# Choosing the experts on the logits, and computing their gates behind the first gathers

## Chip, cores and metric

The kernel runs on one core of a Trainium2 chip. The metric is the device time of one execution in microseconds (us), the median of three runs.

## What is computed

One transformer layer on 16 x 224 = 3584 tokens of 512 values: cross attention on 750 context rows per batch entry, and then a mixture of 8 experts, two per token, each expert taking at most 1120 tokens.

```python
x = x + xattn(layernorm(x), ctx, mask, W_q, W_k, W_v, W_o, b_o)
xf = layernorm(x).reshape(t, D)
probs = softmax(xf @ Wr)
topk_probs, topk_experts = top_k(probs, 2)
for e in range(8):
    mask = topk_experts == e
    gate = sum(where(mask, topk_probs, 0.0))
    vals, idx = top_k(where(any(mask), gate, -inf), cap)      # cap = 1120
    h = relu(xf[idx] @ W1[e]) @ W2[e]                         # 512 -> 2048 -> 512
    y = y.at[idx].add(where(isfinite(vals), vals, 0)[:, None] * h)
x = x + y
```

## The kernel before

**Attention.** `build` first runs `preamble`, which finds from the mask which keys can matter and puts a flag in `T["flag"]`. All engines load that flag and branch: `attention_short` when it is 1, else `attention_general`. The short version is the one that runs on this input. It handles two batch entries in an iteration: the first iteration is written out, six run in a loop, the last is written out. It leaves the router's logits in SBUF, `T["logits"]`, laid out as 112 partitions x 8 experts x 32 token tiles, so 256 columns; the normalized rows go to DRAM as `xn2_rows`. In the instruction streams the branch taken on 1 stands first, the other behind it, and `router` follows.

**Weights.** All products of the experts run as three products on numbers split in a high and a low part. An expert's weights come in 8 pairs of chunks, 1 MB each, through a double buffer `stage`: SyncE loads a pair (`load_pair`), ScalarE writes the high part (`split_pair_hi`, four pieces of 128 x 512), VectorE or GpSimd the low part (`split_pair_lo`, L942). SyncE loads a pair only once the pair two before has its low part. For expert 0, pairs 0 and 1 are loaded in `router` and their high parts made there; GpSimd makes the low parts of pairs 0 to 3, ahead of its first gather, VectorE that of pair 4, and pairs 5 to 7 are split inside block 0 (`refresh`).

**Router** (L945 to L1055). GpSimd makes constant tables with iotas. VectorE waits for all five, copies them, and computes the softmax over the experts (ScalarE does the exponential), then in two rounds the largest probability, its expert (`sel`), and masks it out (`rest`). `has` marks the two chosen experts of each token, `gate` their probabilities. `vals` is a table of four values per token and expert: token number, gate high, gate low, 1. TensorE sums the counts over partitions. If an expert has more than 1120 tokens, `threshold` selects among them by gate; it doesn't run on this input. Each of `router`, `threshold` and `experts` is a block whose end all five engines wait for.

**Slots** (in `experts`). A scan and a product on TensorE give each chosen token its position in its expert (L1349 to L1359, L1477, L1478). VectorE splits the position in a tile number and a row (`slot_tile`, `slot_row`). For an expert, `slot_tiles` compares tile numbers (`eq_t`), `slot_moves` multiplies these with `vals` (`moves`, 1152 columns), and `slot_onehot` makes, eight times, one-hot tables of the rows of four token tiles; TensorE multiplies them (`slot_product`, 4 products of 36 columns each into `psI`), and `slot_ids` turns the result into gather ids, scatter ids and gates. For expert 0 this runs before the first gather; for a later expert it is spread over the 16 steps of the middle block of the expert before (`next_slots`).

**Experts.** An expert has 3 blocks of 3 token tiles, 24 blocks in all. GpSimd gathers the rows of a block from `xn2_rows` by indirect DMA (`xg`), TensorE transposes them (`turn`, `psX`), ScalarE and VectorE write high and low part (`xgT`, `split_x`). A block has 16 steps: TensorE computes `psH` (`hidden`), ScalarE the high part of its relu, VectorE the low part (`hT_lo`, L1390), and TensorE adds the step before to `psY` (`output`). If an expert's counts allow it, a block runs only two of its three tiles. VectorE multiplies `psY` with the gates (`y_out`), GpSimd scatters with addition. VectorE also clears three PSUM banks before block 0 (L1355).

```python
        with nc.If(flag_value(nc, T) == 1):
            attention_short(nc, T, A)
        with nc.Else():
            attention_general(nc, T, A)
```

## Time and profile before

| | |
|---|---|
| median of 3 timed runs | 2272.09 us (2270.47 to 2272.11) |
| profiled execution | 2268.47 us, span 2266.7 us |
| TensorE busy | 2097.9 us (93%) |
| VectorE, ScalarE, GpSimd busy | 994.7 (44%), 677.9 (30%), 511.5 (23%) |
| mean granted TensorE clock | 0.981 of full speed |

The span is what the profiler saw between the first and the last instruction. "Busy" leaves out waits. Idle time of an engine matters only where the chain of work that ends last runs through it. The granted clock is 1.0 at 2.4 GHz and 0.5 at 1.2 GHz.

### The profile page before, as it was taken

What the parts mean: (1) busy time and instruction counts of PE and PEld (TensorE: products, weight loads), DVE (VectorE), ACT (ScalarE), POOL (GpSimd) and SP (SyncE); (2) the same over time, 40 slices, a digit from 0 to 9 for tenths busy, and PEclk for the clock granted to TensorE, in tenths of its full rate; (3) what the DMA queues carried; (4) which work ended last, traced back from release to release, by engine and by line L of the source; (5) the groups of instructions that cost most, each with busy time, mean ns of one, the idle gap of its engine ahead of it and who ended that gap; (6) DMA issues with size and microseconds to landing.
All of it is one profiled execution on the core that took longest, in us unless ns stands there. A gap on an engine that the chain in (4) does not pass through costs nothing.

```text
span 2266.7 us, 30701 instructions
## 1 busy us (share of the span) xinstructions
PE 2097.9 (93%) x12006; PEld 1857.3 (82%) x12006; DVE 994.7 (44%) x2207; ACT 677.9 (30%) x1672; POOL 511.5 (23%) x551
## 2 busy tenths in 40 slices
PE   4898898898896399999999999999999999999997
PEld 3877877877884399899989889998888899988997
DVE  5665666666665633422422342242224345224221
ACT  3533633633542222311321131132113124113110
POOL 1542543543543411110101111010110111110100
PEclk9999999999997599999999999999999999999999
DMA  4122022022012332420421242042124325113211
GB/s 142 48 80 67 13 79 69 11 79 72 7 49 71 120 84 46 133 54 14 119 73 28 46 133 54 14 121 71 28 42 132 60 45 160 27 33 122 41 14 15
DMA packets 95533, 148.40 MB, mean 65 GB/s; under 512 B 7920, under 2 KB 49312, under 8 KB 95376
## 3 DMA queue, kind: packets, MB, share of 16 engines
q1 hardware_dynamic: 79632, 109.36, 15.1%
q0 software_dynamic: 15744, 36.71, 9.2%
q8 instruction: 127, 2.08, 0.4%
q14 instruction: 30, 0.25, 0.0%
HBM read 110.66 MB, written 35.39 MB: 64 GB/s over the span
## 4 chain that ended last, share of the span: by engine, by line
PE 65%; DVE 1%; issue 1%; DMA 0%; POOL 0%; POOLq 0%; ACT 0%; DVEq 0%
PE psH L1410 31%; PE psY L1410 31%; PE psX L1424 1%; PE psI L1455 1%; DMA xg<-xn_rows,gid 0%; DVE onehot L1307 0%; POOL out_dram L1236 0%; POOL xg L1227 0%; DVE moves L1299 0%; POOLq L1157 0%; DVE xg L1349 0%; DVE xg L1369 0%; DVE xg L1352 0%; DVE ys L1364 0%; DVE w_lo L942 0%
## 5 line engine op out<-in xcount | busy, mean ns | idle before, releaser
L1390 DVE SCALAR_TENSOR_TENSOR hT_lo<-psH,hT_hi 128x384 fp32r<-128x384 f32 (+1 forms) x384 | 209.9, 546 | 944.6 <-ACT hT_hi L1266 939.2
L1266 ACT ACTIVATE hT_hi<-psH 128x384 fp32r<-128x384 f32 (+1 forms) x384 | 185.2, 482 | 1124.5 <-PE psH L1410 1119.2
L1410 PE MATMUL psH<-xgT_hi,w_hi 128*128 128x384 f32 (+2 forms) x1536 | 484.8, 316 | 9.5 <-issue 8.8
L1410 PE MATMUL psH<-xgT_lo,w_hi 128*128 128x384 f32 (+2 forms) x1536 | 482.9, 314 | 4.9 <-issue 4.9
L1410 PE MATMUL psH<-xgT_hi,w_lo 128*128 128x384 f32 (+2 forms) x1536 | 484.0, 315 | 0.0
L1410 PE MATMUL psY<-w_hi,hT_hi 128*128 128x512 f32 (+1 forms) x1002 | 402.7, 402 | 0.0
L1410 PE MATMUL psY<-w_hi,hT_lo 128*128 128x512 f32 (+1 forms) x1002 | 394.2, 393 | 0.0
L1410 PE MATMUL psY<-w_lo,hT_hi 128*128 128x512 f32 (+1 forms) x1002 | 394.1, 393 | 0.0
L1410 PEld LDWEIGHTS psH<-xgT_hi,w_hi 128*128 128x128 f32 x1536 | 290.5, 189 | 33.8 <-issue 17.4
L1410 PEld LDWEIGHTS psH<-xgT_lo,w_hi 128*128 128x128 f32 x1536 | 290.6, 189 | 21.0 <-issue 5.7
L1410 PEld LDWEIGHTS psH<-xgT_hi,w_lo 128*128 128x128 f32 x1536 | 290.3, 189 | 0.0
L1227 POOL DMA_INDIRECT xg<-xn_rows,gid x72 | 71.6, 994 | 871.5 <-PE psX L1424 506.5
L1410 PEld LDWEIGHTS psY<-w_hi,hT_lo 128*128 128x128 f32 (+1 forms) x1002 | 187.0, 187 | 43.0
L1236 POOL DMA_INDIRECT out_dram<-ys,sid x72 | 114.5, 1590 | 441.9 <-DVE ys L1336 427.3
L1410 PEld LDWEIGHTS psY<-w_lo,hT_hi 128*128 128x128 f32 (+1 forms) x1002 | 187.9, 188 | 28.7
L1410 PEld LDWEIGHTS psY<-w_hi,hT_hi 128*128 128x128 f32 (+1 forms) x1002 | 188.0, 188 | 27.3
L375 ACT ACTIVATE probs<-probs,nmax 112x250 f32<-112x250 f32 x256 | 126.7, 497 | 111.3 <-DVE nmax L477 111.3
L942 DVE TENSOR_TENSOR w_lo<-stage,w_hi 128x512 fp32r<-128x512 f32 x240 | 154.8, 687 | 1.0 <-ACT w_hi L937 1.0
L937 ACT ACTIVATE w_hi<-stage 128x512 fp32r<-128x512 f32 x256 | 146.1, 624 | 22.2 <-DMA stage<-in_L_ffn_W_dram 22.2
L332 POOL TENSOR_TENSOR probs<-probs,rsum 112x500 f32<-112x500 f32 x128 | 130.6, 1020 | 10.0
L330 POOL TENSOR_TENSOR rsum<-ssum,minus_one 112x2 f32<-112x2 f32 x128 | 89.6, 700 | 131.5 <-ACT probs L375 131.5
L549 PE MATMUL psO<-pT_hi,v_hi 125*128 125x224 f32 x256 | 81.5, 318 | 38.3 <-DVE pT_lo L490 38.3
(187 smaller groups left out, 2965.6 us busy)
## 6 DMA issues: line engine op xcount, KB each, us to landing
stage<-in_L_ffn_W_dram SPq DMA_DIRECT2D x128, 512.0 KB
x_sb<-in_x_dram SPq DMA_DIRECT2D x8, 896.0 KB, 8.1
x_res<-in_x_dram SPq DMA_DIRECT2D x8, 896.0 KB, 5.7
out_dram<-x_res SPq DMA_DIRECT2D x8, 896.0 KB, 4.8
xn_rows<-xn SPq DMA_DIRECT2D x8, 896.0 KB, 4.8
c_sb<-in_ctx_dram SPq DMA_DIRECT2D x16, 375.0 KB
out_dram<-zrow SPq DMA_DIRECT2D x9, 256.0 KB, 4.4
xg<-xn_rows,gid POOLq DMA_INDIRECT x72
```

Source lines behind the costliest of these rows:

```text
L330: nc.gpsimd.tensor_tensor(rsum[:, u % 4, :], ssum[:, u % 4, :], T["minus_one"][0:R, :], ALU.pow).then_inc(recip, 1)
L332: nc.gpsimd.tensor_tensor(P[:, u % 4], P[:, u % 4], rsum[:, u % 4, :].unsqueeze(2).to_broadcast([R, 2, NKEY]), ALU.mult).then_inc(normed, 1)
L375: e = nc.scalar.activation(P[:, i % 4, it, :], P[:, i % 4, it, :], ACT.Exp, bias=nmax[:, i % 4, it:it + 1], scale=-1.0, accum_out=ssum[:, ...
L549: mm = nc.tensor.matmul(out, stationary(a, c), moving(b, c), start=first and c == 0 and j == 0, stop=last and c == n - 1 and j == 2, skip_ ...
L937: nc.scalar.activation(piece(T, 0, pair, j), staged(T, pair, j), ACT.Copy).then_inc(T["w_hi_done"], 1)
L942: engine.tensor_tensor(piece(T, 1, pair, j), staged(T, pair, j), f32(piece(T, 0, pair, j)), ALU.subtract).then_inc(T["w_lo_done"], 1)
L1227: nc.gpsimd.indirect_dma_start(out=xg[0:m, t, :], out_offset=None, in_=A["xn2"], in_offset=bass.IndirectOffsetOnAxis(ap=gid[e % 2][0:m, c: ...
L1236: nc.gpsimd.indirect_dma_start(out=A["out"], out_offset=bass.IndirectOffsetOnAxis(ap=sid[e % 2][0:m, c:c + 1].bitcast(U32), axis=0), in_=y ...
L1266: nc.scalar.activation(hT[0][:, f % 2, 0:m], psH[f % 2][:, 0:m], ACT.Relu).then_inc(h_hi, 1)
L1390: nc.vector.scalar_tensor_tensor(out=hT[1][:, f % 2, 0:m], in0=psH[f % 2][:, 0:m], scalar=0.0, in1=f32(hT[0][:, f % 2, 0:m]), op0=ALU.max, ...
L1410: mm = nc.tensor.matmul(out, stationary(a, c), moving(b, c), start=first and c == chunks[0] and j == 0, stop=last and c == chunks[-1] and ...
L1424: mm = nc.tensor.transpose(psX[c % 2][:, at:at + m], xg[0:m, t, c * 128:(c + 1) * 128], T["ident"][0:m, 0:m])
```

## The change

Seven parts:

1. `build`: the branches are swapped, `attention_general` stands first in the streams and `attention_short` directly ahead of `router`.
2. `router` chooses on the logits (`select`) instead of on the softmax; its VectorE waits first only for one iota, and the other table copies move behind the counts.
3. The ranks (scan, subtraction, two products, `ranks_before`, `positions`) move from `experts` into `router`.
4. The softmax and gates (`gates`, `exponentials`) and the filling of `vals` move into `experts`, behind the ids of expert 0.
5. Position to tile and row: tile numbers stay multiplied by 128, which needs no shift and one cast less (five steps for seven).
6. Expert 0 has an early table of ids only (`early_slots`, `early_ids`, 10 columns); its full table with gates is made in block 0 (`next_slots(0, f)`, `slot_product(0, f - 4)`).
7. GpSimd splits no weights: VectorE makes the low parts of pairs 0 and 1 before block 0; pairs 2 to 7 are split in block 0.

```diff
 build
-            with nc.If(flag_value(nc, T) == 1):
-                attention_short(nc, T, A)
-            with nc.Else():
-                attention_general(nc, T, A)
+            with nc.If(flag_value(nc, T) == 0):
+                attention_general(nc, T, A)
+            with nc.Else():
+                attention_short(nc, T, A)
...
 router, GpSimd
-            for pair in range(EARLY_LO):
-                for j in range(PIECES):
-                    split_pair_lo(nc.gpsimd, T, 0, pair, j)
...
 router, VectorE
+            dve.wait_ge(iotas, 1)
+            nc.vector.tensor_copy(W["rank"][:], rank_i[:])
+            select(dve, nc, T, W, then)
+            then(nc.vector.tensor_tensor(T["has"][:], W["sel"][:, 0], W["sel"][:, 1], ALU.add))
+            nc.vector.tensor_reduce(cnt[:], T["has"][:], AX.X, ALU.add).then_inc(counts, 1)
+            then(nc.vector.tensor_copy(T["keep"][:], T["has"][:]))
+            dve.wait_ge(consts, 5)
+            ranks_before(dve, nc, T, then, marks)
+            dve.wait_ge(counted, 1)
...
 router, ScalarE
-            act.wait_ge(shifted, 1)
-            nc.scalar.activation(z[:], z[:], ACT.Exp).then_inc(exped, 1)
             for pair in range(EARLY):
                 for j in range(PIECES):
                     split_pair_hi(act, nc, T, 0, pair, j)
...
 router, TensorE
             nc.tensor.matmul(ps[0:R, 0:E], T["ones_m"][:], cnt[:], start=True, stop=True).then_inc(counted, 1)
+            positions(pe, nc, T, marks, placed)
+            pe.wait_ge(placed, 1)
...
 experts
-                return (0, BEFORE + f // 2, 2 * (f % 2)) if f < 2 * (WPAIRS - BEFORE) else None
+                return (0, EARLY + f // 2, 2 * (f % 2)) if f < 2 * (WPAIRS - EARLY) else None
...
 experts, GpSimd
-            for pair in range(EARLY_LO, POOL_PAIRS):
-                for j in range(PIECES):
-                    split_pair_lo(nc.gpsimd, T, 0, pair, j)
             gather(0)
...
 experts, ScalarE
-            for pair in range(EARLY, BEFORE):
-                for j in range(PIECES):
-                    split_pair_hi(act, nc, T, 0, pair, j)
+            exponentials(act, nc, T, shifted, exped)
...
 experts, VectorE
+            def early_slots():
+
+                slot_tiles(0)
+                dve.wait_ge(eq_done, 1)
+                nc.vector.tensor_tensor(early_ids[:], eq_t[:], T["ids"][:].unsqueeze(2).to_broadcast([R, NT, EVEN]),
+                                        ALU.mult).then_inc(early_done, 1)
+                for q in range(GROUPS):
+                    slot_onehot(0, 0, q)
+                dve.wait_ge(slot_mm, GROUPS)
+                nc.vector.tensor_copy(gid[0][:], psI[:, 0:CAPT]).then_inc(ids_ready, 1)
...
+            then(nc.vector.scalar_tensor_tensor(out=T["slot_tile"][:], in0=pos, scalar=1.0, in1=T["keep"][:], op0=ALU.add, op1=ALU.mult))
+            then(nc.vector.tensor_scalar(T["pos_i"], T["slot_tile"][:], -1.0, None, ALU.add))
+            then(nc.vector.tensor_scalar(T["row_i"], T["pos_i"], 127, None, ALU.bitwise_and))
+            then(nc.vector.tensor_copy(T["slot_row"][:], T["row_i"]))
+            then(nc.vector.scalar_tensor_tensor(out=flat(T["slot_tile"][:]), in0=flat(T["slot_tile"][:]), scalar=-1.0,
+                                                in1=flat(T["slot_row"][:]), op0=ALU.add, op1=ALU.subtract))
+            early_slots()
             for bank in (*psH, psY[BLK - 1]):
                 s = nc.vector.memset(bank[:], 0.0)
             s.then_inc(cleared, 1)
...
+            gates(dve, nc, T, then_gate, shifted, exped)
...
-            dve.wait_ge(T["w_lo_done"], PIECES * POOL_PAIRS)
-            for pair in range(POOL_PAIRS, BEFORE):
+            for pair in range(EARLY):
                 for j in range(PIECES):
                     split_pair_lo(nc.vector, T, 0, pair, j)
...
+                    if n == 0:
+                        next_slots(0, f)
                     if k == 1 and e + 1 < E:
                         next_slots(e + 1, f)
...
 experts, TensorE
+                    if n == 0 and 4 <= f < 4 + GROUPS:
+                        slot_product(0, f - 4)
```

The new function that chooses:

```python
def select(dve, nc, T, W, then):
    rank, red, eq, sel = W["rank"], W["red"], W["eq"], W["sel"]
    src = T["logits"]
    for k in range(2):
        then(nc.vector.tensor_reduce(red[:, k, :], over_experts(src[:]), AX.X, ALU.max))
        then(nc.vector.tensor_tensor(eq[:], src[:], each_expert(red[:, k, :]), ALU.is_equal))
        then(nc.vector.tensor_tensor(eq[:], eq[:], rank[:], ALU.mult))
        then(nc.vector.tensor_reduce(red[:, 2, :], over_experts(eq[:]), AX.X, ALU.max))
        then(nc.vector.tensor_tensor(sel[:, k], rank[:], each_expert(red[:, 2, :]), ALU.is_equal))
```

After the first round it masks the chosen logit with -BIG, into `rest`, as the code before did with -2.

**How the order moves.** The end of attention on VectorE before (`logits` is the last result, the rows behind the branches are the general version):

```order
L506 COPY x2T<-psT 128x4x112 x4
L510 COPY lgT<-psJ 8x448
L512 COPY logits<-psJ 112x4x8
L199 UNCONDITIONAL_BRANCH
L1558 UNCONDITIONAL_BRANCH
L753 UNCONDITIONAL_BRANCH
L756 UNCONDITIONAL_BRANCH
L756 ISA
L766 TENSOR_SCALAR g_mask_bias<-g_m 112x750
```

and now:

```order
L506 COPY x2T<-psT 128x4x112 x4
L510 COPY lgT<-psJ 8x448
L512 COPY logits<-psJ 112x4x8
L199 UNCONDITIONAL_BRANCH
L1619 UNCONDITIONAL_BRANCH
L1034 UNCONDITIONAL_BRANCH
L1045 CAST rank<-rank_i 112x256
L947 TENSOR_REDUCE red<-logits 112x32
L948 TENSOR_TENSOR eq<-logits,red 112x256
```

The router's first step now follows attention's last one; the general version stands ahead of attention.

The start of the expert block on VectorE before, from the scan to the low parts of a weight pair:

```order
L1349 SCALAR_TENSOR_TENSOR xg<-xg 112x256
L1352 TENSOR_TENSOR xg<-xg 112x256
L1355 MEMSET psH 128x512 x2
L1355 MEMSET psY 128x512
L1359 CAST ys<-psI 112x256
L1361 TENSOR_SCALAR ys<-ys 112x256
L1363 CAST slot_tile<-ys 112x256
L1364 TENSOR_SCALAR ys<-ys 112x256
L1366 CAST xg<-ys 112x256
L1369 SCALAR_TENSOR_TENSOR xg<-xg 112x256
L1372 TENSOR_SCALAR slot_row<-xg 112x256
L1290 TENSOR_TENSOR eq_t<-iota_t,slot_tile 112x288
```

and now, up to the first step of the gates:

```order
L1402 SCALAR_TENSOR_TENSOR slot_tile<-psI,xg 112x256
L1403 TENSOR_SCALAR xg<-slot_tile 112x256
L1404 TENSOR_SCALAR xg<-xg 112x256
L1405 CAST slot_row<-xg 112x256
L1406 SCALAR_TENSOR_TENSOR slot_tile<-slot_tile,slot_row 112x256
L1323 TENSOR_TENSOR eq_t<-iota_t,slot_tile 112x320
L1348 TENSOR_TENSOR early_ids<-eq_t,ids 112x320
L1340 TENSOR_TENSOR onehot<-iota,slot_row 112x512 x8
L1353 CAST gid<-psI 128x9
L1410 MEMSET psH 128x512 x2
L1410 MEMSET psY 128x512
L962 TENSOR_REDUCE ys<-logits 112x32
```

The scan left this place; one copy stands between the one-hot tables and the ids; the PSUM clears and the gates follow behind it.

Block 0 on VectorE now (each `hT_lo` begins a step of the block):

```order
L1436 SCALAR_TENSOR_TENSOR hT_lo<-psH,hT_hi 128x352
L939 TENSOR_TENSOR w_lo<-stage,w_hi 128x2x256 x2
L1436 SCALAR_TENSOR_TENSOR hT_lo<-psH,hT_hi 128x352
L939 TENSOR_TENSOR w_lo<-stage,w_hi 128x512 x2
L1436 SCALAR_TENSOR_TENSOR hT_lo<-psH,hT_hi 128x352
L939 TENSOR_TENSOR w_lo<-stage,w_hi 128x2x256 x2
L1332 TENSOR_TENSOR moves<-eq_t,vals 112x1152
L1436 SCALAR_TENSOR_TENSOR hT_lo<-psH,hT_hi 128x352
L939 TENSOR_TENSOR w_lo<-stage,w_hi 128x512 x2
L1340 TENSOR_TENSOR onehot<-iota,slot_row 112x512
```

In the order before, these steps held `hT_lo` and, for six of them, `w_lo` alone; `moves` and the one-hot tables stood ahead of the block.

## Rows read from the trace of the kernel before

**Rows 1.** Windows view: us; busy (x) PE, PEld, DVE, ACT, POOL; clock; DMA; GB/s.

```profile
722.00:785.00 63.00, 13.70 (x52) 11.48 (x53) 41.44 (x74) 13.21 (x25) 29.84 (x31) 0.51 0.40 129
```

**Rows 2.** Timeline (start, duration, engine, line, operation, idle before): attention ends, router starts.

```profile
721.49 0.21 DVE L512 COPY logits<-psJ 112x32 f32<-112x32 f32 x1 [0.54 <-PE psJ L606]
...
722.15 0.42 SPq L929 DMA_DIRECT2D stage<-in_L_ffn_W_dram  x1
...
722.46 0.38 POOL L973 IOTA rank_i<- 112x256 int32 x1 [11.34 <-POOLq L199]
...
726.29 0.29 DVE L1002 CAST rank<-rank_i 112x256 f32<-112x256 int32 x1 [4.59 <-issue]
```

**Rows 3.** DMA queues, 722 to 724 us: packets, MB, share of 16 engines.

```profile
q14 instruction: 3, 0.02, 3.6%
```

**Rows 4.** DMA queues, 220 to 640 us: all that moved packets.

```profile
q1 hardware_dynamic: 12989, 22.22, 17.6%
```

**Rows 5.** Timeline of the choice of experts: GpSimd, then VectorE.

```profile
730.25 5.49 POOL L942 TENSOR_TENSOR w_lo<-stage,w_hi 128x512 fp32r<-128x512 f32 x4 [6.00 <-ACT w_hi L937]
...
734.66 1.37 DVE L1023 SCALAR_TENSOR_TENSOR rest<-sel,router_probs 112x256 f32<-112x256 f32 x1
...
736.06 0.58 DVE L1016 TENSOR_REDUCE red<-rest 112x32 f32<-112x256 f32 x1
...
738.67 0.42 DVE L1026 TENSOR_TENSOR xg<-sel 112x256 f32<-112x256 f32 x1
```

**Rows 6.** Timeline of VectorE, the ranks in the expert block.

```profile
743.38 1.38 DVE L1349 TENSOR_TENSOR_SCAN xg<-xg 112x256 f32<-112x256 f32 x1 [1.46 <-PEq L947]
744.79 1.30 DVE L1352 TENSOR_TENSOR xg<-xg 112x256 f32<-112x256 f32 x1
746.20 1.03 DVE L1355 MEMSET psH<- 128x512 f32 x2
...
748.23 0.42 DVE L1359 CAST ys<-psI 112x256 int32<-112x256 f32 x1 [0.47 <-PE psI L1478]
```

**Rows 7.** Timeline of ScalarE, the last weight split of the router.

```profile
732.15 2.19 ACT L937 ACTIVATE w_hi<-stage 128x512 fp32r<-128x512 f32 x4 [0.42 <-DMA stage<-in_L_ffn_W_dram]
```

**Rows 8.** Timeline of the slots of expert 0: VectorE, TensorE, VectorE, GpSimd.

```profile
754.23 0.29 DVE L1372 TENSOR_SCALAR slot_row<-xg 112x256 f32<-112x256 f32 x1
...
762.45 5.54 PE L1455 MATMUL psI<-moves,onehot 112*128 112x36 f32 x24 [0.64 <-DVE onehot L1307]
...
768.03 0.20 DVE L1320 COPY slot<-psI 128x36 f32<-128x36 f32 x1 [1.14 <-PE psI L1455]
...
769.73 1.40 POOL L1227 DMA_INDIRECT xg<-xn_rows,gid  x1 [7.88 <-DVE slot L1327]
```

**Rows 9.** Timeline from the gathers to the first product.

```profile
769.33 2.50 DVE L942 TENSOR_TENSOR w_lo<-stage,w_hi 128x512 fp32r<-128x512 f32 x4
...
779.80 1.44 PE L1424 MATMUL psX<-ident,xg 128*128 128x128 f32 x6 [11.81 <-DMA xg<-xn_rows,gid]
...
781.18 1.11 DVE L1283 TENSOR_TENSOR xgT_lo<-psX,xgT_hi 128x352 fp32r<-128x352 f32 x2 [9.35 <-ACT xgT_hi L1255]
...
784.36 0.63 PE L1410 MATMUL psH<-xgT_hi,w_hi 128*128 128x352 f32 x1 [1.16 <-issue]
```

**Rows 10.** Timeline of VectorE in block 1.

```profile
842.13 1.35 DVE L1299 TENSOR_TENSOR moves<-eq_t,vals 112x1152 fp32r<-112x1152 f32 x1
844.47 0.56 DVE L1390 SCALAR_TENSOR_TENSOR hT_lo<-psH,hT_hi 128x384 fp32r<-128x384 f32 x1 [1.00 <-ACT hT_hi L1266]
...
847.29 0.56 DVE L1390 SCALAR_TENSOR_TENSOR hT_lo<-psH,hT_hi 128x384 fp32r<-128x384 f32 x1 [1.66 <-ACT hT_hi L1266]
...
850.55 0.56 DVE L1390 SCALAR_TENSOR_TENSOR hT_lo<-psH,hT_hi 128x384 fp32r<-128x384 f32 x1 [2.10 <-ACT hT_hi L1266]
```

**Rows 11.** Waits after 786 us: who waited for whom, total us, times, longest.

```profile
ACT w_hi L937 <- DMA stage<-in_L_ffn_W_dram: 1.0, 1, 1.0
```

**Rows 12.** Costliest groups: count, busy us, mean ns, idle before.

```profile
L1227 POOL DMA_INDIRECT xg<-xn_rows,gid x72 | 71.6, 994 | 871.5 <-PE psX L1424 506.5
```

More of the change, by code:

```diff
@@ L998, in then @@
                 dve.wait_ge(step, done[0])
-            logits = T["logits"]
+            dve.wait_ge(iotas, 1)
[7 more added lines that the diff above has]
+            dve.wait_ge(counted, 1)
+            then(nc.vector.tensor_reduce(over[:, 0:1], ps[0:1, 0:E], AX.X, ALU.max))
+            then(nc.vector.tensor_scalar(over[:, 1:2], over[:, 0:1], float(CAP) + 0.5, None, ALU.is_gt))
+            then(nc.vector.tensor_copy(T["flag"][:], over[:, 1:2]))
+            for k in range(NBLK):
+                m = nc.vector.tensor_scalar(more[:, :, k], ps[0:1, 0:E], TILES[k][-1] * 128 + 0.5, None, ALU.is_gt)
+            then(m)
+            nc.vector.tensor_copy(T["more"][:], more[:].rearrange("p e k -> p (e k)"))
             dve.wait_ge(iotas, 5)
-            nc.vector.tensor_copy(rank[:], rank_i[:])
             nc.vector.tensor_copy(T["iota"][:], iota_i[:])
@@ L1033, in _ @@
-            dve.wait_ge(counted, 1)
-            for k in range(NBLK):
-                nc.vector.tensor_scalar(more[:, :, k], ps[0:1, 0:E], TILES[k][-1] * 128 + 0.5, None, ALU.is_gt)
-            then(nc.vector.tensor_reduce(over[:, 0:1], ps[0:1, 0:E], AX.X, ALU.max))
-            then(nc.vector.tensor_scalar(over[:, 1:2], over[:, 0:1], float(CAP) + 0.5, None, ALU.is_gt))
-            nc.vector.tensor_copy(T["more"][:], more[:].rearrange("p e k -> p (e k)"))
-            then(nc.vector.tensor_copy(T["flag"][:], over[:, 1:2]))
@@ L1041, in _ @@
[L1041 removed]
+            then(nc.vector.tensor_copy(T["ids"][:], id_i[:]))
         @block.scalar
         def _(act):
[L1045 to L1046 removed]
             for pair in range(EARLY):
@@ L1474, in more @@
                                       max_val=1, skip_runtime_bounds_check_because="it is a comparison's result")
-            pe.wait_ge(marks, 1)
-            nc.tensor.matmul(psI[0:R, 0:E * NT], T["after"][:], flat(T["keep"][:]), start=True, stop=False)
-            nc.tensor.matmul(psI[0:R, 0:E * NT], T["ones_m"][:], flat(before[:]), start=False, stop=True).then_inc(placed, 1)
             for q in range(GROUPS):
-                slot_product(0, q)
+                early_product(q)
             for c in range(DCH):
```

195 lines of the change are left out of this document (103 added, 92 removed).

## Prediction

> **What bounds the kernel now.** I read the busy time by stretches first, then the chain of waits, then each engine's timeline between the end of attention and the first expert block. Attention (to 722 us) and the expert blocks (from 785 us) are TensorE at work. Between them lie 63 us in which TensorE is busy 13.7 us and its granted clock is 0.51, the lower level (1.2 GHz), while VectorE is busy 41 us [rows 1]. In this stretch the chain of waits runs through VectorE's router and slot steps, then the first gathers, then TensorE. Everything after hangs on the moment at which the first `psH` product starts, 784.36 us, and follows at TensorE's pace. So I work out that start anew, then what block 0 gets to do in addition.
>
> **1. Entry to the router.** Attention's last VectorE operation starts at 721.49; SyncE passes the barrier and issues at 722.15, GpSimd makes `rank_i` at 722.46 (0.38 us), but VectorE starts only at 726.29, 4.59 us of "issue" [rows 2]. At that moment instruction packets are fetched [rows 3]: VectorE leaves `attention_short` by a jump over the general version, some 340 rows of its order. The change swaps the two branches, so VectorE falls into the router. Its first operation then needs only `rank_i`: 722.9, 3.4 us earlier. If the stall had another cause, the 3.4 us stay in this step.
>
> The same jump is now taken at the start of the kernel, before attention's first loads are used. Bounds: 0 (target already fetched) and 3.4 us (as at the end). I take 0: six passes of attention's loop, five jumps back on every engine, show no instruction packet at all from 220 to 640 us [rows 4], so a jump to code that is held costs no fetch, and the weight loads that the stalled fetch had beside it are not there yet.
>
> **2. Choosing on the logits.** GpSimd no longer splits weights. Its 5.49 us group from 730.25 on covered part of the choice: the two-input step at 734.66 took 1.37 us, one of the same 256 columns at 738.67, with GpSimd idle, 0.42 [rows 5]. I price all at the second kind. One round of choosing is 736.06 to 738.67 = 2.61 us. Forward from 722.9 (a two-input step counts 0.46, its 0.42 and 0.04 to the next): cast 0.2, two rounds 5.22, masking 0.46, `has` 0.46, count and `keep` 0.76, which gives 730.0. The softmax and the tables of gates are no longer ahead of it. The scan ran 1.38 us beside GpSimd [rows 6]; its bounds are 0.42 and 1.38, I take 0.42 because every other two-input step of this size that I could read both ways fell to it. Scan and subtraction: 0.92, the two position products 2.13 (746.10 to 748.23) [rows 6]: positions at 733.1, at most 734.0.
>
> **3. What is late next.** The router's block ends when all engines reach its end. ScalarE still splits weight pairs 0 and 1 there, and their loads start no earlier than now: its last group starts at 732.15 and takes 2.19 [rows 7], until 734.3. That was hidden (VectorE went on to 741.9); now it is last by 1.2 us. So 1.2 us of step 1 and 2's gain is lost, and an error there under 1.2 us costs nothing. VectorE stood idle 1.46 us between the two blocks (the scan's idle time, [rows 6]); same barrier, same load of the flag, same jump over `threshold`: 735.8.
>
> **4. Slots of expert 0.** Two steps of two inputs at 0.46, three of one input at 0.33 (0.29 and the 0.04 to the next) [rows 8], and two on 320 columns at 0.54: 3.0, so 738.8. The 4-value table `moves` is off this path. Eight one-hot tables follow at the rate of uncontended 512-column subtractions, 2.50 for four [rows 9]: 5.0, and 1.1 from the last to the result (idle time of 1.14, [rows 8]). Bounds: TensorE took 5.54 for 24 products of 36 columns, 0.92 per table [rows 8]; 10 columns cannot take more, so at most 0.7 + 8 times 0.92 = 8.1 in all, at least 6.1. I take 6.1, as the products shrink to 10 columns: 744.9. The ids then need one copy, 0.2 in place of eight small steps, and 0.3 to GpSimd: first gather at 745.4 against 769.73 [rows 8], **24.3 us earlier**.
>
> **5. Behind the gathers.** Gather to turn took 10.1 us (to 779.80), turn to the first product 4.6 [rows 8, 9]. VectorE meanwhile runs three PSUM clears (two took 1.03 [rows 6], so 1.6), the gates (eleven steps and ScalarE's exponential, 0.42 each as in rows 5: 5.1), and now both early pairs' subtractions, 8 at 0.63 = 5.0. From 745.1 it is free at 756.8. It is wanted at 745.4 + 11.45 = 756.85 (781.18 less 769.73) [rows 9]. The two paths are level: cover used up, nothing lost. Faster gathers would gain nothing, a VectorE 1 us later costs 1 us. First product: 760.1, still 24.3 earlier.
>
> **6. Block 0 pays.** The full slot product of expert 0 moves into block 0. In block 1, where such products already stand, the step between `hT_lo` starts is 2.82 us without one (844.47 to 847.29) and 3.26 with one (847.29 to 850.55) [rows 10]: 8 times 0.44 = 3.5. VectorE has now in one step `hT_lo` 0.56, two subtractions 1.3 and `moves` 1.35 [rows 9, 10] = 3.2, 0.4 over 2.82. In the next step its first one-hot table ends 0.5 (ScalarE's half) + 0.56 + 1.3 + 0.7 after the product, and 0.4 late: 3.4 where TensorE asks at 2.8. That is 0.6, once. Together +4.1.
>
> Pairs 2 to 7 are now loaded and split in block 0, two pieces per step. Need: 1 MB in two steps, 5.64 us or more. Supply: 2 MB issued from 722.15 were in at 732.15, 5.0 per pair [rows 2, 7]; in the later experts at the same pace ScalarE waited for a load once, 1.0 us [rows 11]. Cost 0, with about 1 us to spare for each.
>
> **Sum.** -24.3 + 4.1 = **-20.2 us**. The profiled execution took 2268.47 (span 2266.7 and 1.8 around it), 3.6 below the median of the three timed runs, 2272.09. So 2248.3 for such an execution, and **2251.9** against the median.
>
> **Rivals.**
>
> *The jump at the start stalls too.* +3.4 on the path, since VectorE's first statistics open attention. For: the stall at 722 to 726 with its fetch. Against: rows 4. Gives 2255.3. The Trainium skill (Runtime: NRT & Kernel Launch, Instruction fetch mechanics) says that fetching is sequential, that a taken branch out of the two-block window stalls, and that the window is 512 instructions on most engines, 2048 on TensorE. By that rule the target at the start lies inside the window and the cost is 0. No row here shows the window's size.
>
> *Weights late in block 0.* The second gather group now shares the queues with pairs 3 and 4, and a pair's load may start only when the pair two before is subtracted, about 6.5 us ahead of its use. If such a load takes 8.5 us (1.7 MB at 5.0 per MB), each of five pairs is 2 us late: +10. Gives 2261.9.
>
> *Descriptors held up.* GpSimd's gather instruction took 1.40 us beside VectorE's subtractions, on average 0.99 [rows 8, 12]. If each of the three waits 0.5 us behind the copies and casts of the gate steps, the turn is 1.4 later: 2253.3. The Trainium skill (SBUF — State Buffer, Who interferes with whom) says that copies and casts in a two-port mode lock GpSimd out of descriptor writing, so it speaks against computing the gates behind the gathers.
>
> *Contention was not GpSimd's.* If VectorE's steps stay at their long durations, 0.95 us more on each of six such steps of the new path, 5.7 us come back, less the 1.2 of step 3: 2256.4. Against: rows 5.
>
> *Slower: attention's loop refetches.* The swap moves the loop's code by some 340 rows on VectorE, more on TensorE. If it then no longer fits what is held, each of the five jumps back stalls. At 4.6 us, the gap of rows 2, that is 23, and 3.4 for the start: -20.2 + 26.4 = +6.2, 2278.3. It decides from 4.0 us per jump. Against: the loop is no longer than before, and no fetch shows in it now.
>
> **How the numbers follow.** Forecast 0.65; start jump 0.13; weights late 0.10; descriptors 0.04; contention stays 0.04; refetch 0.03; 0.01 for none of these. A measurement here tells 0.2% (4.5 us) from no change. All cases but refetch and the rest are faster by more: 0.94 faster, 0.03 same, 0.03 slower. Range: below, a ScalarE that ends 1.2 earlier, no 0.6 in block 0, and the spread of the medians of about 2 us give 2247; above it reaches to the late weights, 2262.
>
> **What would show it.** VectorE's first router step near 722.9 plus any loss at the start; the router's block ending with ScalarE's pair 1; one-hot tables 0.63 apart; first gather 24 us earlier counted from attention's end; `moves` and eight slot products inside block 0 and steps of 3.3 us. ScalarE waiting for `stage` in block 0, a first attention step later than before, or instruction packets from 220 to 640 us would show me wrong.

## The result, and the profile after

The changed kernel took **2240.13 us** (median of 4 runs, 2237.11 to 2241.82) against 2272.09 before; the ratio is 0.9866 (95% interval 0.9848 to 0.9884). The forecast was 2251.9 with a range of 2247 to 2262: the direction was right, the gain of 32 us is 12 us more than forecast and outside the range. The profiled execution took 2237.11 us (span 2235.4, granted clock 0.987), against 2268.47 (span 2266.7).

I cut both traces at the same eight moments: the first VectorE operation of attention, attention's last `logits`, the router's first operation, the first gather's issue, the first `psH` product of block 0, and the first `ys` of blocks 0, 1 and 23 (each is one row's start, each figure a difference of two starts; the `ys` of a block are made while TensorE is already at the next one).

| stretch, us | before | after | difference | forecast |
|---|---|---|---|---|
| to attention's first VectorE operation | 15.31 | 18.57 | +3.3 | 0 |
| attention, to its last `logits` | 706.2 | 702.2 | -4.0 | 0 |
| to the router's first operation | 4.80 | 0.94 | -3.9 | -3.4 |
| router and slots, to the first gather | 43.4 | 23.2 | -20.2 | -20.9 |
| gather to first product | 14.6 | 14.5 | -0.2 | 0 |
| first product to the first `ys` of block 0 | 52.5 | 57.4 | +4.9 | +4.1 |
| first `ys` of block 0 to that of block 1 | 51.3 | 51.4 | 0.0 | 0 |
| from there to the first `ys` of block 23 | 1366.8 | 1355.6 | **-11.2** | 0 |

The sum is -31.3. The first `ys` of block 0 came 20.15 us earlier, as forecast (-20.2), but partly by luck: the start lost 3.3 us that I had put at nothing, and attention, in which nothing was changed, was 4.0 us shorter. The miss is the last line.

The start and the entry to the router, timeline of VectorE after (start, duration, engine, line, operation, idle before):

```profile
18.57 0.69 DVE L427 BATCH_NORM_STATS2 st<-x_sb 112x6 f32<-112x512 f32 x1 [14.13 <-issue]
...
720.72 0.21 DVE L512 COPY logits<-psJ 112x32 f32<-112x32 f32 x1 [0.54 <-PE psJ L606]
721.65 0.41 DVE L1045 CAST rank<-rank_i 112x256 f32<-112x256 int32 x1 [0.73 <-POOL rank_i L1020]
```

The stall of [rows 2] is gone (0.73 us of idle time in place of 4.59, and its end is GpSimd's `rank_i`), and the start shows one instead: ScalarE and SyncE begin attention at 15.17 us in both kernels, VectorE at 18.57 in place of 15.31, and between 0 and 20 us instruction packets are fetched (two on queue q14, one on q8) where the kernel before has none.

The router and slots on VectorE, then the weights on ScalarE, then the first gather on GpSimd, the turn on TensorE and VectorE's work behind the gather:

```profile
728.77 0.69 DVE L980 TENSOR_TENSOR_SCAN xg<-xg 112x256 f32<-112x256 f32 x1
729.50 0.43 DVE L981 TENSOR_TENSOR xg<-xg 112x256 f32<-112x256 f32 x1
...
733.52 0.42 DVE L1402 SCALAR_TENSOR_TENSOR slot_tile<-psI,xg 112x256 f32<-112x256 f32 x1 [2.28 <-PEq L994]
...
738.15 0.69 DVE L1340 TENSOR_TENSOR onehot<-iota,slot_row 112x512 fp32r<-112x512 f32 x1 [0.51 <-PE psI L1504]
739.00 0.69 DVE L1340 TENSOR_TENSOR onehot<-iota,slot_row 112x512 fp32r<-112x512 f32 x1 [0.16 <-PE psI L1504]
```
```profile
727.12 2.19 ACT L934 ACTIVATE w_hi<-stage 128x512 fp32r<-128x512 f32 x4 [31.37 <-DMA stage<-in_L_ffn_W_dram]
730.10 2.19 ACT L934 ACTIVATE w_hi<-stage 128x512 fp32r<-128x512 f32 x4 [0.79 <-DMA stage<-in_L_ffn_W_dram]
```
```profile
744.88 1.24 POOL L1265 DMA_INDIRECT xg<-xn_rows,gid  x1 [21.66 <-DVE gid L1353]
746.42 0.96 POOL L1265 DMA_INDIRECT xg<-xn_rows,gid  x1 [0.30 <-issue]
```
```profile
751.21 1.44 PE L1472 MATMUL psX<-ident,xg 128*128 128x128 f32 x6 [6.85 <-DMA xg<-xn_rows,gid]
756.74 1.43 PE L1472 MATMUL psX<-ident,xg 128*128 128x128 f32 x6 [4.09 <-DVE xgT_lo L1316]
759.34 0.63 PE L1458 MATMUL psH<-xgT_hi,w_hi 128*128 128x352 f32 x1 [1.16 <-issue]
```
```profile
751.35 4.91 DVE L939 TENSOR_TENSOR w_lo<-stage,w_hi 128x512 fp32r<-128x512 f32 x8
756.17 0.95 DVE L1316 TENSOR_TENSOR xgT_lo<-psX,xgT_hi 128x352 fp32r<-128x352 f32 x2
```

Operations of 256 columns run at their short times (0.43 where [rows 6] had longer ones); the scan takes 0.69. The one-hot tables come 0.85 and 0.95 apart, each held up by TensorE's product. The gather now lands after 6.3 us (10.1 before), and then TensorE waits 4.09 us for VectorE, which is still at the weights.

In the later blocks the difference is idle time of TensorE without a releaser. The groups of instructions between 870 and 2225 us (busy us, mean ns, idle before), of the kernel before, then of the changed one:

```profile
L1410 PE MATMUL psH<-xgT_hi,w_hi 128*128 128x384 f32 (+2 forms) x1400 | 443.7, 317 | 7.8 <-issue 7.1 <-DVE w_lo L942 0.6
L1410 PE MATMUL psH<-xgT_lo,w_hi 128*128 128x384 f32 (+2 forms) x1401 | 442.4, 316 | 4.9 <-issue 4.9
```
```profile
L1458 PE MATMUL psH<-xgT_hi,w_hi 128*128 128x384 f32 (+2 forms) x1400 | 444.2, 317 | 3.4 <-issue 3.3
L1458 PE MATMUL psH<-xgT_lo,w_hi 128*128 128x384 f32 (+2 forms) x1400 | 442.5, 316 | 0.0
```

So 12.0 us of "issue" before and 3.3 after, 8.7 of the 11.2 us; the mean product is the same. In TensorE's timeline of the kernel before they are single gaps (the four longest are shown), two of them in the middle of a group of three products on the same tiles:

```profile
959.56 0.39 PE L1410 MATMUL psH<-xgT_hi,w_hi 128*128 128x256 f32 x1 [2.40 <-issue]
...
1679.88 0.44 PE L1410 MATMUL psH<-xgT_lo,w_hi 128*128 128x384 f32 x1 [1.97 <-issue]
...
1754.78 0.38 PE L1410 MATMUL psH<-xgT_hi,w_hi 128*128 128x256 f32 x1 [1.68 <-issue]
...
1806.06 0.39 PE L1410 MATMUL psH<-xgT_lo,w_hi 128*128 128x256 f32 x1 [2.04 <-issue]
```

The branches that answer to the first and the third in the changed kernel:

```profile
936.41 0.39 PE L1458 MATMUL psH<-xgT_hi,w_hi 128*128 128x256 f32 x1 [0.24 <-issue]
...
1726.78 0.39 PE L1458 MATMUL psH<-xgT_hi,w_hi 128*128 128x256 f32 x1 [1.34 <-issue]
```

Each of them lies within 5 us of a block's end, where TensorE's program branches on `more(n)` or jumps over the variant of the steps that it did not run. TensorE's instructions come as packets on DMA queue q8, and one starts 2.4 to 2.8 us before each of the four gaps ends (at 957.2, 1677.5, 1752.3 and 1803.3). DMA queues around the last gap, 1797 to 1809 us, and around the same place of the changed kernel, 1769 to 1781 us (packets, MB, share):

```profile
q8 instruction: 4, 0.07, 2.2%
```
```profile
q8 instruction: 2, 0.03, 1.0%
```

While blocks 2 to 23 ran, the kernel before fetched 104 packets for TensorE, the changed kernel 98. The two kernels' instructions of one block are the same; what differs is how many stand ahead of it: the early products, and a slot product in both variants of block 0.

**Theory A**: the gaps are instruction fetches, and which branches have one depends on where they stand in the packets that the instructions come in (16 KB each: 127 packets, 2.08 MB on queue q8 of the kernel before). **Rival B**: the earlier gathers and loads, or another part of the change, took contention away. **Rival C**: such gaps vary from one execution to the next.

### The profile page after: what moved, and what is told of

Its sections match the earlier page's. It is cut to its first block, busy times and chain, and to the rows that moved or that the text cites. A ratio compares the mean times of both kernels' runs of the same rounds, so it can differ in the third digit from the quotient of the medians.

```text
span 2235.4 us, 30763 instructions
## 1 busy us (share of the span) xinstructions
PE 2096.5 (94%) x12038; PEld 1860.0 (83%) x12038; DVE 996.3 (45%) x2223; ACT 678.0 (30%) x1672; POOL 488.8 (22%) x535
## 4 chain that ended last, share of the span: by engine, by line
PE 65%; DVE 1%; issue 0%; POOL 0%; POOLq 0%; ACT 0%; DVEq 0%
PE psH L1458 31%; PE psY L1458 31%; PE psX L1472 1%; PE psI L1514 1%; DVE w_lo L939 0%; PE psI L1504 0%; POOL out_dram L1274 0%; POOLq L1196 0%; DVE moves L1332 0%; DVE onehot L1340 0%; DVE psH L1410 0%; DVE hT_lo L1436 0%; DVE ys L1380 0%; DVE ys L965 0%; DVE eq_t L1323 0%
## 5 line engine op out<-in xcount | busy, mean ns | idle before, releaser
L939 DVE TENSOR_TENSOR w_lo<-stage,w_hi 128x512 fp32r<-128x512 f32 x256 | 164.9, 687 | 0.4 <-ACT w_hi L934 0.4
L934 ACT ACTIVATE w_hi<-stage 128x512 fp32r<-128x512 f32 x256 | 146.4, 625 | 32.5 <-DMA stage<-in_L_ffn_W_dram 32.5
```

Of the source, the lines that this page charges most:

```text
L934: nc.scalar.activation(piece(T, 0, pair, j), staged(T, pair, j), ACT.Copy).then_inc(T["w_hi_done"], 1)
L939: engine.tensor_tensor(piece(T, 1, pair, j), staged(T, pair, j), f32(piece(T, 0, pair, j)), ALU.subtract).then_inc(T["w_lo_done"], 1)
```

## Experiments

All times are medians; "against before" is the difference to the kernel before as timed beside it on the same chip (its median was 2268.9 to 2270.6 us there). "Blocks 2 to 23" is the last line of the table above, in the profiled execution.

| run | us | against before | blocks 2 to 23 |
|---|---|---|---|
| before_shift134 | 2268.3 | -2.2 | 1369.7 |
| after_shift122 | 2246.3 | -24.2 | 1361.9 |
| after_order | 2236.5 | -34.0 | 1355.2 |
| before_nopool | 2258.1 | -12.4 | 1373.1 |
| before_shift144 | 2258.3 | -12.3 | 1360.5 |
| after_shift112 | 2249.4 | -21.3 | 1367.6 |
| after_gates_late | 2239.9 | -30.8 | 1356.1 |
| before_nopool_shift144 | 2246.6 | -23.8 | 1359.6 |
| after_again | 2239.1 | -31.3 | 1355.8 |
| after_gates_sp | 2237.9 | -32.5 | 1354.6 |
| after_gates_sp_order | 2238.9 | -31.5 | 1356.4 |
| after_shift32 | 2247.2 | -21.7 | 1360.8 |
| after_shift64 | 2250.0 | -18.9 | 1364.8 |
| after_shift192 | 2252.9 | -16.0 | 1369.8 |
| after_shift224 | 2248.1 | -20.9 | 1365.5 |

### A padding that moved hardly anything

```diff
@@ threshold, TensorE: behind the last product
+            for _ in range(67):
+                nc.tensor.matmul(ps[0:R, E * NT:E * NT + E], T["ones_m"][:], cnt[:], start=True, stop=True)
```

Expected of it in the kernel before:

> The kernel before, with 67 products (134 instructions) added to TensorE's block of the general routing step, which is jumped over and never runs; every instruction of the expert blocks now stands where it stands in the changed kernel from block 1 on. Theory A (the 11 us that the changed kernel gained in blocks 2 to 23 come from where its TensorE branches fall in the instruction fetch): 9 to 11 us faster than the kernel before, all of it in blocks 2 to 23; the gaps of 2.40, 1.97, 1.68 and 2.04 us without a wait at 959.6, 1679.9, 1754.8 and 1806.1 us go, and one of some 1.3 us comes at block 15. Rival B (earlier timing of transfers, less contention): no difference, the gaps stay where they are. Rival C (they vary from one execution to the next): gaps of the same sum at other places.

And of the changed kernel with 61 such products:

> The changed kernel, with 61 products (122 instructions) added in the same block that never runs, so that its expert blocks stand 256 instructions (one packet of 16 KB) behind those of the kernel before. Theory A, if the pattern repeats with the packet: 9 to 11 us slower than the changed kernel, with gaps of 2 us again near the blocks 3, 13, 15 and 16. Rivals B and C: the same time as the changed kernel within 2 us.

Measured: ratio 0.9986 (0.9974 to 0.9998) for the first, with gaps left at blocks 3, 14 and 16 (1.94, 2.10 and 2.59 us); the second 6 us slower than the changed kernel (3.15 us at 1520.05, 1.94 at 2229.19), not at the blocks named. By the letter, theory A was refuted by the first. But the instruction packets told that the edit had not done what I meant: they came where they came before it in a block, to within 2 us. The cause stands in the traces: a product of plain float32 runs as two passes (one product of `positions`, and the one of the counts, each have two rows), each a weight load and a product. So 67 products take 268 places and 61 take 244, and with a packet of 256 instructions that is a shift of +12 and of -12: the two packets inside block 2 started 0.1 and 1.1 us earlier in the one kernel and 1.9 and 1.1 us later in the other. (The Trainium skill, Runtime: NRT & Kernel Launch, Instruction fetch mechanics, gives blocks of 16 KiB with 256 instructions; the trace agrees.) Theory A was hardly tested, though the second run has gaps of 1.94 and 3.15 us that no profile of the changed kernel has.

### The same padding at the right size

36 products (144 places) in the kernel before, 28 (112 places) in the changed one; nothing else.

> The first padding was nearly a whole packet: the rows show a product of plain float32 as two passes, so 67 products took 268 places in the instruction stream, 12 more than the 256 of a 16 KB packet, and the packets of TensorE's instructions came 0.1 to 1.1 us earlier in a block, where those of the changed kernel come 11 us later. This is the kernel before with 36 such products (144 places) in the general routing step that never runs, so that the packets fall in each expert block as in the changed kernel (45.6 us behind the start of block 2's third part in place of 35.1). Theory A (the 11 us in blocks 2 to 23 come from where the branches stand in the packets): 9 to 11 us faster than the kernel before, all in blocks 2 to 23. Rival B (transfers and their timing, the other parts of the change): no faster, gaps of about 2 us stay at blocks 3, 13, 15 and 16.

> The changed kernel with 28 such products (112 places) in the step that never runs, so that the packets fall as in the kernel before. Theory A: 9 to 11 us slower than the changed kernel, in blocks 2 to 23, with gaps of about 2 us near the starts of blocks 3, 13, 15 and 16. Rival B: the changed kernel's time within 2 us.

The packets went where they were meant to: behind the first `ys` of block 1, one starts 35.1 us later in the kernel before, 45.1 with the padding, 45.6 in the changed kernel, 35.2 in the changed kernel with its padding. That of the padded kernel before, DMA queues from 929.5 to 931.5 us (packets, MB, share):

```profile
q8 instruction: 1, 0.02, 4.0%
```

The kernel before became 12.3 us faster (ratio 0.9955, 0.9937 to 0.9974) by instructions that never run. "All in blocks 2 to 23" was not so: these took 6.3 us less in the profiled execution, whose whole span was 9.3 us shorter (attention 2.4, the router and slots 0.9 of it), and the rest of the 12.3 is not located. The packets fetched in blocks 2 to 23 fell from 104 to 98, the gaps at blocks 13 and 16 went, those at blocks 3 and 15 shrank from 2.40 and 1.68 us to 1.22 and 1.00. At block 3:

```profile
954.51 0.39 PE L1412 MATMUL psH<-xgT_hi,w_hi 128*128 128x256 f32 x1 [1.22 <-issue]
```

The changed kernel with the padding became 9 to 10 us slower, with 12.0 us more in blocks 2 to 23, most of it at blocks 3, 13, 14 and 16. In block 3:

```profile
937.71 0.28 PE L1460 MATMUL psH<-xgT_hi,w_lo 128*128 128x256 f32 x1 [3.09 <-issue]
```

Here 104 packets came in blocks 2 to 23. Theory A holds from both sides, and rival B falls for this part: the transfers, the other engines' programs and the order of the work are the same in each pair. Rival C falls as the whole cause, since the medians moved beyond their intervals both times. But it holds in part: single executions of the kernel before took 2262.3 to 2275.1 us, and its version without splits on GpSimd (below), with the same TensorE program and the same 104 packets, took 1373.1 us in blocks 2 to 23 where the kernel before took 1366.8. And the two profiles of the changed kernel show 0.24 and 0.85 us of "issue" at block 3. How long a stall lasts varies from one execution to the next.

A gap can cost more than itself. In the run before_shift134 the granted clock fell to 0.5 for 3.4 us and for 6.8 us at the gaps of blocks 14 and 16, and block 16 took 57.2 us, in place of 51.3 without a gap. Not every gap does this, and its length alone does not decide it: the clock stayed at 1.0 through the gaps of 1.97 to 2.40 us of the kernel before and through those of 3.15 and 3.17 us in after_shift122 and after_shift64, and fell for 3.4 us at one of 1.77 us in after_shift112.

### The circle of positions

The changed kernel with 8, 16, 48 and 56 such products (32, 64, 192 and 224 places).

> The changed kernel with 8 products of plain float32 (32 places) in the general routing step that never runs. Theory A: the time goes by where the branches stand in the packets, most positions cost less than that of the kernel before: 2240 to 2246 us, and the packets come 3 us earlier in each block. Rival (only the position of the kernel before is bad): 2237 to 2242 us.

> The same with 16 products (64 places). Theory A: between the changed kernel and its version with 112 places (2249 us), 2240 to 2250 us, packets 6.5 us earlier in each block. Rival: 2237 to 2242 us.

> The same with 48 products (192 places), 64 places short of a whole packet. Theory A: 2237 to 2250 us, packets 6.5 us later in each block than in the changed kernel. Rival: 2237 to 2242 us.

> The same with 56 products (224 places), 32 places short of a whole packet. Theory A: by the run with 244 places (2246 us, 6 us above the changed kernel, though its packets came only 1 us later) 2242 to 2248 us. Rival: 2237 to 2242 us, and the 2246 us were another chip's.

With the runs above, by places behind the changed kernel, modulo 256: 2239 and 2240 us at 0, 2247 at 32, 2250 at 64, 2249 at 112, 2253 at 192, 2248 at 224, 2246 at 244. Those at 32 and 192 were 1 and 3 us over what theory A had been given, the other two at its upper end; the rival's 2237 to 2242 is out for all, and so is another chip as the reason, since the kernel before took 2268.9 us beside these four and 2270.5 beside the run at 244. The changed kernel stands at the best of the seven positions tried, the kernel before (near 110) among the bad ones. The blocks that lose most change: 0 and 3 at 32, 9 and 18 at 64, 3 and 16 at 112, 4 and 15 at 192, 10 and 21 at 224. At 32 the longest gap of all runs, 3.96 us, stands in block 0, which took 3.9 us more there to its first `ys` than in the changed kernel (61.3 for 57.4); the table's last column does not have it. The packets fetched in blocks 2 to 23 were 98 in all eight kernels at or near 0, 103 or 104 in the four at 110 to 122, and 101, 105, 102, 100 and 97 at 32, 64, 192, 224 and 244. So they go with the time, but roughly. At 192, TensorE's groups between 818 and 2240 us:

```profile
L1460 PE MATMUL psH<-xgT_hi,w_lo 128*128 128x384 f32 (+2 forms) x1465 | 463.4, 316 | 4.1 <-issue 4.1
L1460 PE MATMUL psH<-xgT_hi,w_hi 128*128 128x384 f32 (+2 forms) x1464 | 463.3, 316 | 10.1 <-issue 9.9
```

Why a given position stalls at a given branch stays open.

### No weight splits on GpSimd, alone

```diff
-EARLY_LO = 1
-POOL_PAIRS = 4
-BEFORE = 5
+EARLY_LO = 0
+POOL_PAIRS = 0
+BEFORE = 2
...
-            dve.wait_ge(T["w_lo_done"], PIECES * POOL_PAIRS)
```

> The kernel before with one part of the change alone: no weight splits on GpSimd (VectorE makes the low parts of pairs 0 and 1 ahead of block 0, the others are made in block 0 as in the changed kernel). As I priced the contention (router and slot operations of 0.4 us that took 1.25 to 1.4): the router's and the slots' VectorE work shrinks by some 13 us and the first gather is issued near 757 in place of 769.7; block 0 gives 4 us back, so 8 to 9 us faster in all. Rival (the contention was not GpSimd's splits but the loads' writes): operations stay at 1.25 to 1.4 us, no gain, and 4 us slower.

Measured 12.4 us faster (ratio 0.9938, 0.9921 to 0.9954). From the router's first operation to the gather it took 31.8 us in place of 43.4. The second group of GpSimd's splits in the kernel before, and three position steps on VectorE beside it:

```profile
748.75 5.17 POOL L942 TENSOR_TENSOR w_lo<-stage,w_hi 128x512 fp32r<-128x512 f32 x4 [0.31 <-ACT w_hi L937]
...
749.02 1.25 DVE L1363 CAST slot_tile<-ys 112x256 f32<-112x256 int32 x1
750.18 1.35 DVE L1364 TENSOR_SCALAR ys<-ys 112x256 int32<-112x256 int32 x1
751.57 1.23 DVE L1366 CAST xg<-ys 112x256 f32<-112x256 int32 x1
```

The scan (1.38 us in [rows 6]) and the same three steps now, at short times:

```profile
738.79 0.69 DVE L1349 TENSOR_TENSOR_SCAN xg<-xg 112x256 f32<-112x256 f32 x1 [1.46 <-PEq L947]
...
742.87 0.29 DVE L1363 CAST slot_tile<-ys 112x256 f32<-112x256 int32 x1
743.08 0.28 DVE L1364 TENSOR_SCALAR ys<-ys 112x256 int32<-112x256 int32 x1
743.40 0.29 DVE L1366 CAST xg<-ys 112x256 f32<-112x256 int32 x1
```

So the contention was GpSimd's: it went with GpSimd's splits. The edit also takes the loads and high parts of pairs 2 to 4 out of this stretch, and no weights are loaded during the short steps shown, so these rows alone would leave the loads as a rival. Two others do not. In the kernel before, the step of 1.37 us of [rows 5] ran beside GpSimd with no transfer at all; in the changed kernel, steps of 0.42 us ran with the DMA queues full and GpSimd idle (PE, PEld, DVE, ACT, POOL busy, clock, DMA share, GB/s):

```profile
734.60:735.70 1.10, 0.00 (x0) 0.00 (x0) 1.07 (x2) 0.00 (x0) 1.10 (x1) 0.50 0.00 0
```
```profile
724.00:726.00 2.00, 0.00 (x0) 0.00 (x0) 1.86 (x5) 0.00 (x0) 0.00 (x0) 0.50 1.08 359
```
And block 0 took 52.8 us to its first `ys` (52.5 before): making pairs 2 to 7 in block 0 costs nothing. The expectation's "block 0 gives 4 us back" was wrong; the 5 to 6 us that block 0 takes longer in the changed kernel (57.4 and 58.3) come with the slot table, as the forecast had it (by elimination: no run has the table alone); some of it is again "issue" (0.96 and 0.37 us for 0.55 in the kernel before). With the packets moved as well:

> The kernel before with two edits at once: no weight splits on GpSimd, and 36 products (144 places) in the general routing step that never runs. If the two gains are apart from one another (12.4 us for the first alone, 12.3 us for the second alone): 24 to 25 us faster than the kernel before, 2246 us; what the changed kernel is faster than that (some 6 us) is the worth of all its reordering of the router and the slots. Rival (one gives back what the other won, both being about transfers): 2250 us or more.

Measured 23.8 us faster (ratio 0.9896): the two gains add up. Beside it on the same chip the changed kernel took 2239.1, so all its reordering is worth 7.5 us. The traces have it as -8.6 (router and slots, 31.8 to 23.2), -4.1 (entry), +3.4 (start), +5.7 (block 0), -0.8 (attention and the gather) and -3.8 in blocks 2 to 23, in whose TensorE steps the reordering changed nothing: why they are shorter is open.

### The order of the branch

```diff
-            with nc.If(flag_value(nc, T) == 0):
-                attention_general(nc, T, A)
-            with nc.Else():
-                attention_short(nc, T, A)
+            with nc.If(flag_value(nc, T) == 1):
+                attention_short(nc, T, A)
+            with nc.Else():
+                attention_general(nc, T, A)
```

> The changed kernel with the order of the first branch undone: the short attention first, the general one in the Else. If the jump is what VectorE waited for: its first operation of the attention back from 18.6 us to 15.3 (3.3 us won), and the 3.4 us jump back at its end, before the router, so 0 to 1 us slower or faster in all, with a gap of about 4.6 us from the last attention operation to the router's first in place of 0.73. Rival (the stall at the start is hidden by the loads of x and the attention catches up, since the logits stood only 0.8 us apart at the end): about 3.9 us slower.

Attention starts at 15.26 us again, and the gap before the router is back, 5.35 us from start to start in place of 0.94. Swapping the branches thus wins 4.4 and costs 3.3: a stall moved, not removed. Attention took 700.9 us here, and 699.6 to 706.2 over all profiled executions, 702.2 and 704.4 in two of the same kernel. So a difference of a few us in attention says nothing. By the medians (2236.5 against 2240.1) the edit won 3.6 us; made once more, on after_gates_sp below, it lost 1.0 (2238.9 against 2237.9). A gain is not shown.

### VectorE's order behind the gather

```diff
+            for pair in range(EARLY):
+                for j in range(PIECES):
+                    split_pair_lo(nc.vector, T, 0, pair, j)
+            for c in range(DCH):
+                split_x(0, c)
             gate_steps = [0]
...
-            for pair in range(EARLY):
-                for j in range(PIECES):
-                    split_pair_lo(nc.vector, T, 0, pair, j)
-            for c in range(DCH):
-                split_x(0, c)
```

ScalarE's exponentials stand behind its x parts in turn.

> The changed kernel with VectorE's work between the gather's issue and its landing put in another order: the low parts of weight pairs 0 and 1 first, then x's low parts, and the gates (5.2 us) behind them, ScalarE's exponentials behind its x parts. VectorE is then free when the gather has landed at 751.2 and TensorE's wait of 3.8 to 4.1 us before its third turn goes. Theory: block 0's first product 4 us earlier, the first h_lo not over 0.5 us late, so 3.5 to 4 us faster than the changed kernel. Rival: the gates push h_lo and the first slot table back, TensorE waits for them in block 0 and 2 us or less remain.

> The changed kernel once more, beside the two next on the same chip: 2237 to 2242 us.

In after_gates_sp, SyncE first waits for that gather:

```diff
+            sp.wait_ge(gathered, 16 * BLK)
             for e in range(E):
                 for pair in range(EARLY if e == 0 else 0, WPAIRS):
```

> The changed kernel with the gates behind x's low parts, as in the run before; there the weights' low parts, made early, let SyncE load pairs 2 and 3 (1.0 MB) into the gather, which landed 9.2 us after its issue in place of 6.3, and no time was won. Here SyncE also waits for that gather before it loads pair 2. Theory: the gather lands after 6.3 us again, TensorE's third turn waits 0.5 us, block 0's first product comes 14.5 us after the gather's issue in place of 14.5 + 3.3, and the whole is 3 to 4 us faster than the changed kernel. Rival: pair 2 comes too late for block 0, and TensorE or ScalarE waits there for as long.

And with the order of the branch undone as well:

> The same, with the short attention first in the branch as before the change (the start's stall of 3.3 us goes, one of some 4.4 us comes back ahead of the router). By the two traces 0.4 us faster to 1.1 us slower than the run before this one; by the medians of the changed kernel with and without that edit (2236.5 against 2240.1) up to 3.6 us faster.

The wait of 4.09 us went (0.52 to 0.53 in all three), and almost nothing was won. In after_gates_late the gather landed 9.2 us after its issue, beside 0.8 MB of weights, and the product came 13.7 us after it. In after_gates_sp it landed after 6.8, and the product came 11.4 us after it, 3.1 less than in the changed kernel. But from there to the first `ys` took 59.6 us in place of 57.4 and 58.3 (the two profiles of the changed kernel): TensorE stood still at the first branch of block 0,

```profile
763.20 0.39 PE L1459 MATMUL psH<-xgT_hi,w_hi 128*128 128x256 f32 x1 [2.33 <-issue]
```

and the clock, which had risen at 760.3, fell again from 763.7 to 767.1. Stretches of this run (PE, PEld, DVE, ACT, POOL busy, clock, DMA share, GB/s), then of the changed kernel:

```profile
760.00:763.00 3.00, 0.87 (x5) 0.57 (x3) 2.68 (x8) 1.50 (x3) 0.00 (x0) 0.96 0.64 249
763.00:767.00 4.00, 3.80 (x16) 3.50 (x17) 2.00 (x5) 1.19 (x3) 0.00 (x0) 0.58 0.03 8
```
```profile
760.00:763.00 3.00, 3.00 (x11) 2.74 (x10) 0.00 (x0) 0.00 (x0) 1.61 (x2) 0.53 0.84 295
763.00:767.00 4.00, 2.71 (x17) 2.28 (x17) 2.54 (x5) 2.73 (x6) 0.00 (x0) 1.00 0.19 71
```

1.3 us are left by the medians (2237.9 against 2239.1), within their spread. Of the three, none beats the changed kernel by more than that spread. In both runs where the first product came some 3 us sooner, the stall at the branch of block 0 was longer: 2.33 and 1.95 us for 0.96 and 0.98 in the changed kernel.

## Why the prediction fell short

1. **Entry to the router, and the start.** The size at the end was about right (3.9 for 3.4), the start was not: "I take 0" was wrong, it is 3.3 us, near the upper bound, and the rival at 0.13. The argument from [rows 4] was about jumps to code that had just run; it says nothing of a first jump ahead. The Trainium skill (Runtime: NRT & Kernel Launch, Instruction fetch mechanics) has a window of 512 instructions, by which a jump over some 340 rows stays inside; the trace disagrees here, with 3.26 us.
2. **Choosing on the logits.** Right: all steps fell to 0.42 to 0.58. Only the scan was mis-sized, 0.69 for 0.42.
3. **What is late next.** ScalarE's pair 1 ended the router's block as forecast, but at 732.3, not 734.3, since the loads landed sooner; 1.0 us later than VectorE's own last step.
4. **Slots of expert 0.** 23.2 us from the router's first step for 22.5: the tables came 0.90 apart on average, held by TensorE, where I took the lower bound of 0.63. The upper bound, 0.92, was the better value: 10 columns in place of 36 did not make a product faster.
5. **Behind the gathers.** The gather landed 3.8 us sooner than I took from before, so the two paths were not level: VectorE was last by 4.09 us, and "faster gathers would gain nothing" was exactly so. The first product still came 14.5 us behind the gather's issue, for 14.7 forecast.
6. **Block 0.** +4.9 for +4.1, and weights cost nothing, as said. The wait for the one-hot table was 0.27 us, not 0.6, and 0.8 us of "issue" at and behind the branch was in no term.
7. **The step that failed: "everything after follows at TensorE's pace".** I took blocks 1 to 23 as unchanged because their code is. That left out that a longer program ahead of them moves every branch in the instruction packets. These blocks were 11.2 us shorter in the trace, and moving the packets alone was worth 9 to 12 us by the medians of the two padded pairs. In the profiles it was 6.3 and 12.0 us, and the last 5 us are not explained by position: the padded kernel before still took 1360.5 us in blocks 2 to 23, the changed one 1355.6 (the changed one's packets inside block 2 started 0.2 and 0.5 us later; other parts of the change were not tried apart).

Of the rivals, the start's stall happened. Weights were not late, contention did not stay (before_nopool), attention's loop did not refetch (one instruction packet from 220 to 640 us), and the gathers' instructions took 1.24, 0.96 and 0.94 beside the clears and the gates. Two slips changed nothing: with 3.4 us for the start, refetching would have had to cost 3.4 us per jump, not 4.0, to use up the gain, and the chances of the cases called faster add up to 0.96, not 0.94.

Without the luck of position the change is worth some 19 to 21 us, close to the 20.2 of the sum: 19.0 beside the padded kernel before (31.3 less 12.3), 21.3 with its own padding beside the kernel before. Of these, 12 come from taking the splits off GpSimd, some 8 from the reordering. That it is so close is luck in part, since the start's loss and the 5 us in blocks 2 to 23 were in no term.

## What to carry to other kernels

A change that adds or removes instructions on the engine that sets the pace, ahead of long unrolled code with branches, can move the time by 10 us in 2240, as here, with no bearing on its merit. Before crediting or blaming an edit for a gain in blocks that it did not touch, look there for idle time marked "issue" at the branches, and run the old kernel once with padding that never executes, checking in the packets that it moved what it should. A swap of two branches moves a jump from one place to another, so count its stall at both. And a wait removed just ahead of another stall gave little here.

## What the runs showed of the hardware

- Instructions come in 16 KB packets, one each 22 to 26 us in the middle of TensorE's blocks and some 3 us apart at their ends. Within 5 us of branches over about 570 to 730 instructions TensorE stood still for up to 4.0 us, and for how long depended on the program's position modulo 256 instructions: 2239 to 2253 us over seven positions, with the same work. The Trainium skill (Runtime: NRT & Kernel Launch, Instruction fetch mechanics) gives TensorE a window of 2048 instructions, in which all these targets would lie; the trace disagrees, with gaps of 1 us and more at every position tried.
- Gaps of 2.1 and 2.6 us between dense products were followed by a granted clock of 0.5 for 3.4 and 6.8 us, one of 1.77 us by 3.4 us of it, while two of 3.15 and 3.17 us left it at 1.0.
- A float32 product of 256 or of 8 columns shows two rows, and 36 of 8 columns moved the packets by 10 us, near the 10.5 us of 144 places (by 24 us for 256, a packet comes 13.5 us earlier and so the next one 10.5 later). The scan took 0.69 us where two-input steps of the same size take 0.42.
- A gather landed 6.3 and 6.8 us after its issue with the queues to itself, and 9.2 us with 0.8 MB of weights beside it.
- VectorE's steps of 0.29 us on 256 columns took 1.23 to 1.35 us beside GpSimd's subtractions, and 0.28 to 0.29 once GpSimd made none; the DMA queues had no part in it (a slow step at DMA share 0.00, fast ones at 1.08).
